# Last pass of a graph network on one core: two layers from split parts, splits 14 pieces ahead, low parts by whole blocks

## The reference, cut to what matters

```python
x = _layernorm(x + relu(adj @ x @ K + b))          # x: 4096x128, adj: 4096x4096, fp32
u, v = x, v0
for _ in range(3):
    v = mlp(adj @ u, uv_W1, uv_b1, uv_W2, uv_b2, uv_W3, uv_b3)
    u = mlp(adj @ v, vu_W1, vu_b1, vu_W2, vu_b2, vu_W3, vu_b3)
return _layernorm(x + v)
```

## Time and profile before

| what | value |
|---|---|
| median of 3 runs | 1170.84 us (1170.68 to 1171.25) |
| the profiled execution's own time | 1170.68 us |
| its span, first to last instruction | 1168.8 us |
| busy TensorE, VectorE, ScalarE | 1154.0, 738.1, 660.9 us |
| granted TensorE clock, mean | 0.999 of full |
| read from HBM | 258.61 MB |

### The profile page before, as it was taken

How to read it: one execution, slowest core, us unless ns; L and a number is a source line. 1 busy time by engine, 2 the same in 40 slices (tenths; PEclk the granted TensorE clock), 3 DMA queues, 4 the chain that set the end, 5 groups by cost and what they waited for, 6 DMA issues and landing times.

```text
span 1168.8 us, 13697 instructions
## 1 busy us (share of the span) xinstructions
PE 1154.0 (99%) x5236; PEld 953.2 (82%) x5236; DVE 738.1 (63%) x890; ACT 660.9 (57%) x809; POOL 0.2 (0%) x4
## 2 busy tenths in 40 slices
PE   7999999999999999999999999999999999999997
PEld 6888888888888888888888888888888888887776
DVE  7997676458564555555545746554566555678884
ACT  7765555346554555555444754554556444667874
POOL 0000000000000000000000000000000000000000
PEclk9999999999999999999999999999999999999999
DMA  9988785568366646555656736655665555589870
GB/s 383 406 302 321 247 271 191 206 215 288 125 205 210 216 161 224 189 184 180 216 180 216 250 116 223 207 179 178 207 225 184 195 200 214 188 296 362 297 261 36
DMA packets 72209, 261.60 MB, mean 224 GB/s; under 512 B 8016, under 2 KB 8656, under 8 KB 71120
## 3 DMA queue, kind: packets, MB, share of 16 engines
q1 hardware_dynamic: 72000, 260.61, 63.6%
q10 hardware_dynamic: 144, 0.13, 0.0%
HBM read 258.61 MB, written 2.10 MB: 223 GB/s over the span
## 4 chain that ended last, share of the span: by engine, by line
PE 93%; DMA 3%; DVE 2%; ACT 1%; issue 0%; SPq 0%; DVEq 0%; ACTq 0%
PE agg_ps L892 28%; PE agg_ps L885 28%; PE agg_ps L878 28%; PE pre_ps L789 4%; DMA adj_raw<-in_adj 3%; PE hid_ps L750 1%; PE hid_ps L752 1%; PE hid_ps L751 1%; DVE adj_lo L742 1%; ACT adj_hi L613 1%; PE hid_ps L811 1%; PE hid_ps L825 0%; ACT feat_hi L613 0%; DVE stats L626 0%; ACT resid L528 0%
## 5 line engine op out<-in xcount | busy, mean ns | idle before, releaser
L742 DVE TENSOR_TENSOR adj_lo<-adj_raw,adj_hi 128x1024 fp32r<-128x1024 f32 x464 | 548.1, 1221 | 226.4 <-ACT adj_hi L613 221.0
L878 PE MATMUL agg_ps<-adj_hi,feat_hi 128*128 128x512 f32 x1484 | 587.0, 396 | 7.5 <-ACT adj_hi L613 7.5
L885 PE MATMUL agg_ps<-adj_hi,feat_lo 128*128 128x512 f32 x1484 | 579.4, 390 | 0.0
L613 ACT ACTIVATE adj_hi<-adj_raw 128x1024 fp32r<-128x1024 f32 x464 | 468.3, 1052 | 86.0 <-PE agg_ps L892 72.4
L892 PE MATMUL agg_ps<-adj_lo,feat_hi 128*128 128x512 f32 x1484 | 458.8, 390 | 0.2 <-DVE adj_lo L742 0.2
L878 PEld LDWEIGHTS agg_ps<-adj_hi,feat_hi 128*128 128x128 f32 x1484 | 279.6, 188 | 66.4 <-issue 9.8
L885 PEld LDWEIGHTS agg_ps<-adj_hi,feat_lo 128*128 128x128 f32 x1484 | 279.5, 188 | 59.7 <-issue 2.4
L892 PEld LDWEIGHTS agg_ps<-adj_lo,feat_hi 128*128 128x128 f32 x1484 | 278.9, 188 | 59.6 <-DVE adj_lo L742 1.1
L507 ACT ACTIVATE hid<-hid_ps,params 128x512 f32<-128x512 f32 (+1 forms) x80 | 54.5, 681 | 61.0 <-PE hid_ps L752 50.6
L578 ACT ACTIVATE in_hi<-part 128x512 fp32r<-128x512 f32 x24 | 15.2, 634 | 110.4 <-DVE part L731 110.4
L507 ACT ACTIVATE post<-pre 128x512 f32<-128x512 f32 x39 | 24.6, 631 | 79.8 <-DVE pre L709 79.8
(11 more groups left out here) (78 smaller groups left out, 382.3 us busy)
## 6 DMA issues: line engine op xcount, KB each, us to landing
adj_raw<-in_adj SPq DMA_DIRECT2D x472, 512.0 KB, 5.6
adj_raw<-in_adj SPq DMA_DIRECT2D x8, 1024.0 KB, 8.1
resid<-in_x SPq DMA_DIRECT2D x8, 256.0 KB, 8.1
out<-resid SPq DMA_DIRECT2D x7, 256.0 KB, 5.5
params<-in_weights SPq DMA_DIRECT2D x1, 386.0 KB, 4.7
b_row<-in_bias_rows SPq DMA_DIRECT2D x1, 128.0 KB, 5.6
out<-resid ACTq DMA_DIRECT2D x1, 128.0 KB, 2.1
out<-resid SPq DMA_DIRECT2D x1, 128.0 KB, 2.2
```

Source lines behind the costliest of these rows:

```text
L613: act.activation(split_hi(b)[:, i * CHUNK:(i + pieces) * CHUNK], adj_raw[:, h % RAW, 0:pieces * CHUNK], ACT.Copy).then_inc(adj_hi_ready, 1)
L742: dve.tensor_tensor(split_lo(b)[:, slot], adj_raw[:, h % RAW, 0:pieces * CHUNK], split_hi(b)[:, slot].bitcast(F32), ALU.subtract).then_inc ...
L878: pe.matmul(group_bank(g), feat_hi[feats][:, tile(src, i)], split_hi(b)[:, piece(i)], start=start, stop=False)
L885: pe.matmul(group_bank(g), feat_lo[feats][:, tile(src, i)], split_hi(b)[:, piece(i)], start=False, stop=False)
```

## The change

For four rows of the last pass (0, 7, 6, 5) a new table LAST_PARTS takes the place of LAST: both hidden layers are made from parts, and the steps have other places. TensorE has layer 1 eight ticks after completion (four before), layer 2 at 16 (7) and pe_out at 20 (9). On VectorE and ScalarE everything from dve_pre on moves to later ticks, and stands closer together: pre, post, total and statistics at 21, 22, 23, and std, shift, normalisation at 26, 27, 28 (before: 12, 15, 15 and 20, 20, 24). Splits of the last pass are due 14 ticks ahead, not 20. VectorE makes the low part of a last-pass block in one instruction of 128x2048 when its second half is due, in place of two of 128x1024, and signals both halves at its end.

```diff
--- before.py
+++ after.py
@@ -38,11 +38,12 @@
          ("both", 6, (5,)))
 WHOLE = 8
 HOLD = 3
-LEAD, FIRST_LEAD, LAST_LEAD, FIRST_ROWS = 12, 4, 20, 3
+LEAD, FIRST_LEAD, LAST_LEAD, FIRST_ROWS = 12, 4, 14, 3
 LOAD_GCN, LOAD_PARAMS = 24, 90
 W_SPLIT = 320
 
-IN_PARTS, TURN, LATE2, LATE, END, END2 = "in_parts", "turn", "late2", "late", "end", "end2"
+IN_PARTS, TURN, LAST_PARTS, LATE2, LATE, END, END2 = "in_parts", "turn", "last_parts", "late2", "late", "end", "end2"
+LAST_IN_PARTS = 4
 STEPS = {
     GCN: dict(act_in=0, pe_out=3, dve_pre=3, dve_stats=5, act_std=7, dve_norm=9, act_feat=11, dve_feat=12),
     IN_PARTS: dict(dve_sum=0, act_in=1, dve_in=2, pe_hid1=6, act_hid1=7, dve_hid=9, pe_hid2=13, act_hid2=14,
@@ -51,6 +52,8 @@
                pe_out=12, dve_pre=12, act_post=15, dve_feat=17),
     LAST: dict(dve_sum=0, act_in=0, pe_hid1=4, act_hid1=7, pe_hid2=7, act_hid2=9, pe_out=9, dve_pre=12,
                act_post=15, dve_stats=15, act_std=20, dve_shift=20, act_norm=24),
+    LAST_PARTS: dict(dve_sum=0, act_in=1, dve_in=2, pe_hid1=8, act_hid1=9, dve_hid=10, pe_hid2=16, act_hid2=17,
+                     pe_out=20, dve_pre=21, act_post=22, dve_stats=23, act_std=26, dve_shift=27, act_norm=28),
     LATE2: dict(dve_sum=0, act_in=1, pe_hid1=4, act_hid1=5, pe_hid2=6, act_hid2=7, pe_out=8, dve_pre=10,
                 act_post=10, dve_stats=12, act_std=14, dve_shift=15, act_norm=16),
     LATE: dict(dve_sum=0, act_in=1, pe_hid1=1, act_hid1=2, pe_hid2=3, act_hid2=5, pe_out=5, dve_pre=7, act_post=7,
@@ -214,6 +217,10 @@
 
         return TILES if b in self.first_spare else pieces
 
+    def low_at_once(self, b):
+
+        return self.order[self.first_use(b)][0] == PASSES - 1
+
     def first_use(self, b):
         return next(n for n, of in enumerate(self.block) if of == b)
 
@@ -242,7 +249,8 @@
             return GCN
         if s == PASSES - 1:
             after = len(self.units) - len(END_UNITS) - u
-            return END2 if after < 0 else END if after == 0 else LATE if after == 1 else LATE2 if after == 2 else LAST
+            return END2 if after < 0 else END if after == 0 else LATE if after == 1 else LATE2 if after == 2 \
+                else LAST_PARTS if u < self.rows * (PASSES - 1) + LAST_IN_PARTS else LAST
         return TURN if r in (0, self.rows - 1) else IN_PARTS
 
     def on_vector(self, u):
@@ -251,7 +259,7 @@
 
     def in_parts(self, u):
 
-        return self.steps_of(u) in (IN_PARTS, TURN)
+        return self.steps_of(u) in (IN_PARTS, TURN, LAST_PARTS)
 
     def count_in_parts(self, u):
         return sum(self.in_parts(i) for i in range(u + 1))
@@ -710,13 +718,13 @@
                                       b_row[:, b * P:(b + 1) * P].rearrange("p (j f) -> p j f", f=P)
                                       .to_broadcast([P, len(tiles_of(u)), P]), ALU.add)\
                        .then_inc(pre_ready, 1)
-                u = at(t, "dve_hid", HIDDEN)
+                u = at(t, "dve_hid", DEEP)
                 if u is not None:
                     dve.wait_ge(hid_hi_ready, plan.count_in_parts(u))
                     dve.wait_ge(hid1_ready, deep(u) + 1)
                     dve.tensor_tensor(hid_lo[:, :], hid1[:, :], hid_hi[:, :].bitcast(F32), ALU.subtract)\
                        .then_inc(hid_lo_ready, 1)
-                u = at(t, "dve_in", HIDDEN)
+                u = at(t, "dve_in", DEEP)
                 if u is not None:
                     dve.wait_ge(in_hi_ready, plan.count_in_parts(u))
                     dve.tensor_tensor(in_lo[:, :], agg(u), in_hi[:, :].bitcast(F32), ALU.subtract)\
@@ -737,11 +745,19 @@
                         dve.wait_ge(x_hi_ready, plan.xs.index(c) + 1)
                         dve.tensor_tensor(feat_lo[0][:, columns(c)], resid[:, columns(c)],
                                           feat_hi[0][:, columns(c)].bitcast(F32), ALU.subtract).then_inc(x_lo_ready, 1)
+                    h += 1
+                    if plan.low_at_once(b):
+                        if i == 0:
+                            continue
+                        raw = adj_raw[:, (h - 2) % RAW:(h - 2) % RAW + 2, :].rearrange("p k f -> p (k f)")
+                        dve.wait_ge(adj_hi_ready, h)
+                        dve.tensor_tensor(split_lo(b), raw, split_hi(b).bitcast(F32), ALU.subtract)\
+                           .then_inc(adj_lo_ready, 2)
+                        continue
                     slot = slice(i * CHUNK, (i + pieces) * CHUNK)
-                    dve.wait_ge(adj_hi_ready, h + 1)
-                    dve.tensor_tensor(split_lo(b)[:, slot], adj_raw[:, h % RAW, 0:pieces * CHUNK],
+                    dve.wait_ge(adj_hi_ready, h)
+                    dve.tensor_tensor(split_lo(b)[:, slot], adj_raw[:, (h - 1) % RAW, 0:pieces * CHUNK],
                                       split_hi(b)[:, slot].bitcast(F32), ALU.subtract).then_inc(adj_lo_ready, 1)
-                    h += 1
 
         @block.tensor
         def _(pe):
```

## The result

The changed kernel takes **1184.34 us** (median of 4 runs, 1184.18 to 1184.91) against 1170.76 (1170.57 to 1171.25): ratio 1.0117, 95% interval 1.0104 to 1.0130. It is 13.6 us slower. The profiled execution has a span of 1183.1 us.

The account below looks back on a forecast made before the run. TensorE, busy 1154.0 of 1168.8 us, was taken as the bound. Products (-1.4), old stops removed (-1.7) and new stops (+15.5) added 12.4 us to 1170.7, giving 1183.1 us; stated range 1167.6 to 1187.

Parts of the forecast that it names:

- Products: On TensorE, a product of three costs 0.70 us against 0.88 for an fp32 layer; eight save 1.4 us.
- Whole blocks: On VectorE, one 128x2048 low-part subtraction takes 2.20 us; 36 blocks save 2.5 us.
- Row 6: TensorE stops 5.1 us ahead of the first layer, waiting for in_lo, and 3.5 us more for hid_lo.
- Row 5: TensorE waits 1.1 us for in_lo and 1.9 us for hid_lo.
- Row 4: ScalarE's late steps stop TensorE 2.4 us for hid1, then 1.5 us more behind normalisation and a half block.
- Sum: Products -1.4, old stops -1.7 and new stops +15.5 give +12.4 us, so 1183.1 us.
- Rival 3, the clock: TensorE's clock falls in the 5.1 us stop, costing 0 to 2.4 us: 1183 to 1186; 0.70 shared with the walk.
- Rival 1, the queues keep up: VectorE and ScalarE run further ahead into row 7, all hand-overs land in time: 1167.6 to 1169.3 us; chance 0.18.
- the walk: Step-by-step timing of three engine queues from 1064.3 us: 1183.1 us, own range 1174 to 1187; 0.70 with clock variant.
- the 2.7 us wait behind row 0's normalisation: VectorE waits 2.7 us for a high half that ScalarE makes only after row 0's normalisation, ahead of row 6's sum.
- what matters is the order: VectorE's and ScalarE's added work fits in the totals; their queue order, with 4.75 us between sum and product, makes stops.
- my lower bound for the stop: If no ScalarE wait holds VectorE, row 6's product is late by 0.4 us and its second layer by nothing.

Follow-up runs that it names:

- fill: The changed kernel with 47 added matmuls, results overwritten at once, where TensorE stops at rows 6, 5 and 4: 1184.40 us.
- gaps: The changed kernel with deviation, shift and normalisation of the four rows at 28, 28 and 32 pieces, not 26, 27 and 28: 1173.57 us.
- two_parts: The changed kernel with only rows 0 and 7 in parts, rows 6 and 5 back in fp32 at the old places: 1182.59 us.
- old_places: The changed kernel with all four rows in parts, at nearly the places of the old table: 1184.57 us.
- tuned: gaps with row 4's steps moved and the four rows' statistics, deviation, shift and normalisation at 25, 30, 30 and 34 pieces: 1179.62 us.
- stats_late: The changed kernel with statistics, deviation, shift and normalisation of the four rows at 27, 29, 30 and 32 pieces, not 23, 26, 27 and 28: 1185.13 us.

## Why the prediction came out right, and where it didn't

The forecast was 1183.1 us, the measurement 1184.34, 1.2 more.

- *Products.* 0.70 forecast, 0.70 to 0.71 in the five of the eight that stand behind no stop.
- *Whole blocks.* 2.20 forecast; blocks in a row start at 1111.84, 1114.04 and 1116.24 (the step after), 2.20 apart.
- *Row 6.* First stop 5.1 forecast, 5.08 measured. Second 3.5 against 2.14 (1109.63 less 1107.49): a slow stretch of the clock lay ahead of it and took 1.67 of the time in which TensorE would have waited. In fill, with a full clock, that stop is 3.88 (half block's excess less the product's 0.71).
- *Row 5.* 1.1 and 1.9 forecast; 0 and 1.33 measured, 1.0 and 1.95 in fill.
- *Row 4.* 2.4 forecast, 2.42 measured. The 1.5 at the output was a wait for ScalarE in the forecast; in the changed kernel the excess over pe_out's own 0.91 is 1.42, nearly all of it slow clock, and in fill 1.65, of waiting.
- *Sum.* 15.5 us of stops forecast; fill, where the clock takes no part, has 5.12 + 3.88 + 1.02 + 1.95 + 2.52 + 1.65 = 16.1. What is missing besides: 0.35 at the last chunk of the pass before and 0.32 at row 7's output, where I had found no stop, and 0.46 us ahead of 1037 us.
- *Rival 3, the clock.* It fell, three times and not once, for some 3.4 us each, 0.4 to 0.9 us after TensorE restarted from stops of 5.1, 2.1 and 2.4 us. Each costs some 1.7 us on TensorE, and by fill nothing in the sum. So the measured time lies in this rival's range (1183 to 1186), but not because of the clock. The Trainium skill ("TensorE: Matmul & The Clock Gate", "Why this matters for your kernels") tells one to keep gaps between bursts short; the traces agree that the falls follow gaps, and fill shows no gain from closing them.
- *Rival 1, the queues keep up.* Wrong as forecast. gaps comes nearer to it with three numbers changed, but stays 4.3 us above its range.
- *Range.* A third of 15.5 us of stops gives 1172.8 by the same sum, not the 1174 at the lower end of the walk's own range. The stated range is not touched by it.

**Where the reasoning was wrong.** The walk found the 2.7 us wait behind row 0's normalisation (measured 2.74), and then gave the stop to the 4.75 us of work between sum and product, "what matters is the order". gaps has the same work in the same place and stops 1.4 us, and two_parts hasn't row 6's subtractions and stops 9.5 at its second layer. The step that failed is the reading of the cause. In gaps the product is 1.59 us late by the measure that gives 5.08 here (1095.86 less 1093.81 less 0.46), so the two engines' waits for each other were 3.5 of the 5.1 us; my lower bound for the stop, with those waits gone, was 0.4. The time came within 1.2 us because the walk held these waits; the cause that I named for it played no part in that. The distances of 3, 1 and 1 pieces stood in the diff, and I never weighed them by themselves. That two engines work in turn is shown by the waits and the busy shares; why exactly each table falls into or out of step was read from timelines of single runs, and wasn't derived as a rule.

## What to carry to other kernels

Where two in-order queues hand work to each other, look at the distance between a step and the one that answers it, and count how much other work stands between. In the changed kernel both idled in turn though neither was full: in the changed stretch VectorE was busy 97 of 120 us and ScalarE 87, with blocks of 2.2 us and half blocks of 1.0 us as their long instructions. The runs give no rule for the distance: 5, 0 and 4 pieces worked in gaps and not in old_places or tuned. A timeline walk can hit the time and name the wrong cause; move a suspected distance alone before changing amounts of work. And measure an edit beside its companions: whole blocks gave 2.3 us at one lead and cost 6.0 at another.

## What the runs showed of the hardware

The granted clock fell to its lower level, 1.2 GHz, in the middle of an otherwise full kernel, behind TensorE's stops of 5.1, 2.1 and 2.4 us; behind the 1.3 us stop at row 5 it stayed at 2.4 GHz. With matmuls in the stops it never fell. The length of the stop alone doesn't decide: behind stops of 2.87 us (stats_late, row 6's first layer) and 2.51 us (tuned, row 6's second), both longer than two of those three, the clock of the next 4 us is 1.00.

In a kernel that waits on other engines anyway the falls cost nothing (1184.40 against 1184.34 us), which I had not expected of three falls of some 1.7 us. Where no later stop takes it up, a fall may well show. gaps has one, behind the stop at row 4's second layer (clock 0.51 from 1134.8 to 1138.3 us), and TensorE has no stop after it. Its eight executions took 1172.56 to 1172.94 us (four) and 1174.20 to 1174.65 us (four), with mean granted clocks of 0.998 or 0.999 in the first group and 0.997 or 0.998 in the second, which the profile belongs to. That this fall is the 1.7 us between them is not shown, as none of the first group was profiled.
